# Down products in three f16 parts and reciprocals spread by transfers, in the second layer of a two-layer block

## The reference, cut to what matters

```python
# attention: 16 heads of 64 columns, causal
y = softmax(q k^T / 8) v ;  attn = y @ w_out
# experts: scores of a gate, the top 8 of 16 kept and normalized, one shared expert
hg = xn w_gate[e]^T ; hu = xn w_up[e]^T
h  = silu(hg) * hu
ye = h w_down[e]^T
y  = sum_e ye * combine[e]          # the shared expert with weight 1
out = x + attn + y
```

## Time and profile before

| | |
|---|---|
| median of 3 runs | 3251.74 us (3250.49 to 3253.42) |
| profiled execution | 3248.36 us, its span 3246.6 us |
| layer 0 | up to about 1243 us of the span |
| busy | PE 96%, DVE 62%, ACT 50%, POOL 39% |
| DMA | 259.86 MB, mean 80 GB/s |

### The profile page before, as it was taken

The page is one execution under the profiler, slowest core; times in us unless marked ns, Lnnn a source line. Parts: engine busy times, 40 slices in busy tenths (PEclk is TensorE's granted clock), DMA queues, the critical chain, the costliest instruction groups (busy, mean ns, idle before and its releaser), DMA issues.

```text
span 3246.6 us, 62545 instructions
## 1 busy us (share of the span) xinstructions
PE 3103.6 (96%) x23476; PEld 1674.8 (52%) x23476; DVE 2005.2 (62%) x3829; ACT 1632.8 (50%) x3433; POOL 1279.7 (39%) x1223
## 2 busy tenths in 40 slices
PE   4999999999999994999999999999999999999999
PEld 2565555655555652445555554554554554554554
DVE  5666666656666653666666666666666666666664
ACT  2666656556666663444444444444444444444443
POOL 1333333323333321444444444444444444444444
PEclk9999999999999996999999999999999999999999
DMA  4211122221222113332432432432432442432431
GB/s 116 53 50 50 50 59 63 62 50 50 62 50 52 50 47 107 105 96 76 108 103 71 108 104 71 108 105 70 108 103 72 108 107 68 108 107 68 108 105 43
DMA packets 239643, 259.86 MB, mean 80 GB/s; under 512 B 27248, under 2 KB 228080, under 8 KB 230640
## 3 DMA queue, kind: packets, MB, share of 16 engines
q1 hardware_dynamic: 217680, 239.12, 28.1%
q10 hardware_dynamic: 21664, 16.73, 1.7%
HBM read 107.91 MB, written 21.50 MB: 40 GB/s over the span
## 4 chain that ended last, share of the span: by engine, by line
PE 56%; DVE 2%; DMA 1%; SPq 1%; ACT 1%; POOL 0%; issue 0%; DVEq 0%; POOLq 0%; ACTq 0%
PE l_ps_out L1548 9%; PE l_ps_any L1585 7%; PE l_ps_any L1448 6%; PE l_ps_any L1450 6%; PE l_ps_any L1449 6%; PE l_ps_exp L1531 4%; PE l_ps_exp L1533 4%; PE l_ps_any L1591 3%; PE l_ps_any L1506 3%; PE l_ps_sum L1559 2%; PE l_ps_any L1571 2%; PE l_ps_exp L1535 2%; DMA l_spread<-route_scratch 1%; SPq L1089 1%; PE l_ps_any L1511 1%; PE l_ps_any L1442 1%
## 5 line engine op out<-in xcount | busy, mean ns | idle before, releaser
L1161 POOL TENSOR_TENSOR l_hw<-l_hidden,l_spread 128x512 f32<-128x512 f32 x256 | 325.5, 1277 | 761.5 <-DMA l_spread<-route_scratch 200.2
L614 DVE TENSOR_REDUCE neg_max<-ps_any 128x1 f32<-128x384 f32 (+3 forms) x704 | 417.4, 634 | 269.1 <-PE ps_any L728 264.6
L1249 ACT ACTIVATE l_probs<-l_ps_exp 128x512 f32<-128x512 f32 x640 | 376.9, 596 | 377.4 <-PE l_ps_exp L1535 288.0
L501 ACT ACTIVATE probs<-ps_exp 128x512 f32<-128x512 f32 x640 | 349.3, 602 | 155.2 <-PE ps_exp L743 154.5
L442 POOL TENSOR_SCALAR_AFFINE_SELECT probs<-probs 128x512 f32<-128x512 f32 x256 | 159.4, 634 | 597.4 <-ACT probs L501 597.4
L1370 DVE TENSOR_REDUCE l_neg_max<-l_ps_any 128x2 f32<-128x768 f32 (+2 forms) x384 | 316.4, 863 | 86.4 <-PE l_ps_any L1511 86.0
L1531 PE MATMUL l_ps_exp<-l_q_a,l_k_a 128*128 128x512 f16 (+3 forms) x1024 | 306.4, 300 | 0.3 <-ACT l_probs L1249 0.2
L1548 PE MATMUL l_ps_out<-l_probs,l_v 128*64 128x512 f32 (+3 forms) x2048 | 303.1, 438 | 0.0
L1533 PE MATMUL l_ps_exp<-l_q_b,l_k_b 65*128 65x512 f16 (+3 forms) x1024 | 295.4, 300 | 0.0
L726 PE MATMUL ps_any<-k_st,q_st 120*128 120x128 f16 (+3 forms) x1024 | 252.8, 304 | 36.2 <-DMA k_st<-stack_scratch 35.2
L1256 ACT ACTIVATE l_tanh<-l_ps_any 128x512 f32<-128x512 f32 x272 | 162.4, 597 | 208.2 <-PE l_ps_any L1450 113.7
(11 more groups left out here) (234 smaller groups left out, 6276.1 us busy)
## 6 DMA issues: line engine op xcount, KB each, us to landing
l_spread<-route_scratch SPq DMA_DIRECT2D x64, 1024.0 KB, 5.5
l_q_a<-l_q_hi SPq DMA_DIRECT2D x256, 128.0 KB, 2.4
l_q_b<-l_q_lo SPq DMA_DIRECT2D x128, 128.0 KB, 2.4
l_k_a<-l_k_hi SPq DMA_DIRECT2D x128, 128.0 KB, 2.4
l_k_a<-l_k_lo SPq DMA_DIRECT2D x128, 128.0 KB, 2.4
l_k_b<-l_k_hi SPq DMA_DIRECT2D x128, 128.0 KB, 2.4
q_st<-rot_hi SPq DMA_DIRECT2D x64, 128.0 KB
k_st<-rot_hi SPq DMA_DIRECT2D x64, 128.0 KB
```

The source lines that it names most:

```text
L501: nc.scalar.activation(probs[:, n % 2, u], ps_exp[:, (10 * g + u) % 3], ACT.Exp, scale=float(HD0 + DR) ** -0.5).then_inc(exp_done.sem, 1)
L614: nc.vector.tensor_reduce(neg_max[:, n % 2, heads[0]:heads[0] + k, t], src, AX.X, ALU.max, negate=True).then_inc(drained["dve"], 1)
L1161: nc.gpsimd.tensor_tensor(dst, hidden[:, k % 2], spread[:, c % 2, n % CHUNK], ALU.mult).then_inc(hw_ok.sem, 1)
L1249: nc.scalar.activation(probs[:, n % 2, u], ps_exp[:, (5 * p + u) % ST_BANKS], ACT.Exp, scale=float(HD1) ** -0.5).then_inc(exp_done.sem, 1)
```

## The change

The down weights are split as the gate and up weights are, and `hw` holds two f16 halves. A new step `hw n` comes behind POOL's multiplication: ACT writes the high half, DVE subtracts it from the f32 value and writes the low half. `down` then has three f16 products for each expert, and DVE divides by the weights' scale of 64 while it adds. One ring of five f32 tiles, `hid`, takes the place of `tanh`, `gated` and `hidden`, and is written in place. Routing weights come in chunks of two experts with three buffers.

`rec_lo` and `spread` are gone. `rec_out s` writes the reciprocals of four pairs to DRAM (128 KB), `rec_in` reads those of two pairs back, each row broadcast to the 64 partitions of its head (two transfers of 256 KB) into one buffer, and `divide n` is a DVE product of `yT` with it. The list ORDER1 is another one; the steps are as listed.

```diff
+SPREAD = 2
+HID_SLOTS = 5
 ORDER1 = (
...
+    ("spread_in", 0, 4), ("exp", 0, 0, 3), ("exp", 0, 0, 4), ("rec_in", -1, 2), ("sums", -1, 6), ("rec", -1, 1),
+    ("sums", -1, 7), ("v", 0, 3, 0), ("values", -1, 7), ("max", 0, 1, 0), ("max", 0, 1, 1), ("exp", 0, 1, 0),
+    ("exp", 0, 1, 1), ("max", 0, 1, 2), ("exp", 0, 1, 2), ("max", 0, 1, 3), ("values", 0, 0), ("max", 0, 1, 4),
+    ("up_in", 0, 5), ("gate_in", 0, 6), ("exp", 0, 1, 3), ("up_in", 0, 6), ("v", 0, 0, 1), ("turn_max", 0, 1),
+    ("qk", 0, 2, 0), ("gate_in", 0, 7), ("divide", -1, 4), ("qk", 0, 2, 1), ("exp", 0, 1, 4), ("sums", 0, 0),
+    ("divide", -1, 5), ("hw", 0, 5), ("hw", 0, 6), ("up_in", 0, 7), ("exp", 0, 2, 0), ("qk", 0, 2, 2),
+    ("exp", 0, 2, 1), ("qk", 0, 2, 3), ("exp", 0, 2, 2), ("exp", 0, 2, 3), ("max", 0, 2, 0), ("hw", 0, 7),
+    ("down", 0, 1), ("max", 0, 2, 1), ("gate_in", 0, 8), ("up_in", 0, 8), ("divide", -1, 6), ("exp", 0, 2, 4),
+    ("exp", 0, 3, 0), ("values", 0, 1), ("max", 0, 2, 2), ("gate_in", 0, 9), ("rec_in", -1, 3), ("up_in", 0, 9),
+    ("res", -1), ("exp", 0, 3, 1), ("max", 0, 2, 3), ("load", 1), ("norm", 1), ("hw", 0, 8), ("exp", 0, 3, 2),
+    ("divide", -1, 7), ("sums", 0, 1), ("spread_in", 0, 5), ("hw", 0, 9), ("exp", 0, 3, 3), ("values", 0, 2),
...
+    ("rec_out", 0, 0), ("down", 0, 2), ("hw", 0, 12), ("qk", 0, 3, 2), ("qk", 0, 3, 3), ("exp", 0, 4, 2),
+    ("rec", 0, 0), ("exp", 0, 4, 3), ("gate_in", 0, 14), ("v", 0, 3, 1), ("exp", 0, 4, 4), ("hw", 0, 13),
...
+    ("exp", 0, 7, 1), ("exp", 0, 7, 2), ("gate_in", 1, 4), ("exp", 0, 7, 3), ("max", 1, 0, 4), ("values", 0, 6),
+    ("spread_in", 1, 2), ("qk", 1, 1, 0), ("exp", 0, 7, 4), ("turn_max", 1, 0), ("hw", 1, 1), ("out", 0, 0),
...
+    ("v", 1, 2, 0), ("qk", 1, 1, 3), ("rec_out", 0, 1),
 )
...
+        rec_dram = nc.dram_tensor("rec_scratch", [2, P, T // 2], F32, kind="Internal").ap()
...
-        w_d = sb("w_d", [P, EXPERTS, D])
+        w_d = sb("w_d", [P, 2, EXPERTS, D], F16)
...
-        rec_p = sb("rec_p", [P, 2, T // 2], F16)
-        spread = sb("spread", [P, 2, CHUNK, T])
+        y_rec = sb("y_rec", [P, 2, 2, T // 2])
+        spread = sb("spread", [P, 3, SPREAD, T])
...
-        tanh = sb("tanh", [P, 2, T])
-        gated = sb("gated", [P, T])
-        hidden = sb("hidden", [P, 2, T])
-        hw = sb("hw", [P, HW_SLOTS, T])
+        hid = sb("hid", [P, HID_SLOTS, T])
+        hw = sb("hw", [P, HW_SLOTS, 2, T], F16)
...
-        split_late = [(w_g, w_g_in), (w_u, w_u_in)]
+        split_late = [(w_g, w_g_in), (w_u, w_u_in), (w_d, w_d_in)]
...
+                if name == "rec_out":
+                    k = 2 * b + n
+                    sp.wait_ge(rec_ok.sem, rec_ok.at(k, 2))
+                    if k >= 2:
+                        release(sp, sp_passed)
+                        sp.wait_ge(rec_in.sem, rec_in.at(2 * k - 2, 0))
+                    sp.dma_start(rec_dram[k % 2], rec[:]).then_inc(rec_out.sem, 16)
+                if name == "rec_in":
+                    k = 4 * b + n
+                    sp.wait_ge(rec_out.sem, rec_out.at(k // 2, 16))
+                    if k:
+                        release(sp, sp_passed)
+                        sp.wait_ge(y_div.sem, y_div.at(2 * k, 0))
+                    rows = rec_dram[k // 2 % 2].rearrange("(r f j) q -> r f j q", r=2, f=2)
+                    for r in range(2):
+                        sp.dma_start(y_rec[HD1 * r:HD1 * r + HD1],
+                                     rows[r, :, 2 * (n % 2):2 * (n % 2) + 2].partition_broadcast(HD1)
+                                     ).then_inc(rec_in.sem, 16)
...
+                if name == "hw":
+                    k = EXPERTS * b + n
+                    if k >= HW_SLOTS:
+                        b_old, e_old = divmod(k - HW_SLOTS, EXPERTS)
+                        filling(act, f"d{b_old}_{chunk_of(e_old)}")
+                    act.wait_ge(weighted.sem, weighted.at(k, 1))
+                    nc.scalar.activation(hw[:, k % HW_SLOTS, 0], hid[:, k % HID_SLOTS], ACT.Copy).then_inc(hw_hi.sem, 1)
...
-                if name == "spread":
-                    bank = full(dve, f"spread{b}_{n}")
-                    dve.wait_ge(y_ok.sem, y_ok.at(PAIRS * b + n, 1))
-                    nc.vector.scalar_tensor_tensor(out=yT[:, n], in0=bank, scalar=1.0 / REC_SCALE, in1=yT[:, n],
-                                                   op0=ALU.mult, op1=ALU.mult).then_inc(drained["dve"], 1)
+                if name == "divide":
+                    p = PAIRS * b + n
+                    dve.wait_ge(y_ok.sem, y_ok.at(p, 1))
+                    dve.wait_ge(rec_in.sem, rec_in.at(p // 2, 32))
+                    y = yT[:, n].rearrange("p (f q) -> p f q", f=2)
+                    nc.vector.tensor_tensor(y, y, y_rec[:, :, n % 2], ALU.mult).then_inc(y_div.sem, 1)
...
+                if name == "hw":
+                    k = EXPERTS * b + n
+                    dve.wait_ge(hw_hi.sem, hw_hi.at(k, 1))
+                    nc.vector.tensor_tensor(hw[:, k % HW_SLOTS, 1], hid[:, k % HID_SLOTS], hw[:, k % HW_SLOTS, 0],
+                                            ALU.subtract).then_inc(hw_ok.sem, 1)
...
-                        ins = pe.matmul(out, w_d[:, e], hw[:, k % HW_SLOTS], start=(e == todo[0]), stop=(e == todo[-1]))
+                        for cw, cx in ((0, 0), (0, 1), (1, 0)):
+                            ins = pe.matmul(out, w_d[:, cw, e], hw[:, k % HW_SLOTS, cx],
+                                            start=(e == todo[0] and cw + cx == 0), stop=(e == todo[-1] and cw == 1))
```

More of the change, by code:

```diff
@@ new lines @@
+    ("scale", 1), ("max", 0, 2, 4), ("sums", 0, 2), ("out", -1, 1), ("turn_max", 0, 2), ("exp", 0, 3, 4),
+    ("gate_in", 0, 10), ("outT", -1), ("up_in", 0, 10), ("spread_in", 0, 6), ("qk", 0, 3, 0),
+    ("gate_in", 0, 11), ("exp", 0, 4, 0), ("hw", 0, 10), ("exp", 0, 4, 1), ("up_in", 0, 11), ("qk", 0, 3, 1),
+    ("xnT", 1), ("gate_in", 0, 12), ("up_in", 0, 12), ("sums", 0, 3), ("spread_in", 0, 7), ("hw", 0, 11),
+    ("route", 1), ("v", 0, 1, 1), ("gate", 1), ("gate_in", 0, 13), ("v", 0, 2, 1), ("up_in", 0, 13),
@@ new lines @@
+    ("rec_out", 0, 0), ("down", 0, 2), ("hw", 0, 12), ("qk", 0, 3, 2), ("qk", 0, 3, 3), ("exp", 0, 4, 2),
+    ("rec", 0, 0), ("exp", 0, 4, 3), ("gate_in", 0, 14), ("v", 0, 3, 1), ("exp", 0, 4, 4), ("hw", 0, 13),
+    ("max", 0, 3, 0), ("values", 0, 3), ("max", 0, 3, 1), ("exp", 0, 5, 0), ("sums", 0, 4), ("max", 0, 3, 2),
+    ("exp", 0, 5, 1), ("rec_in", 0, 0), ("exp", 0, 5, 2), ("max", 0, 3, 3), ("divide", 0, 0), ("up_in", 0, 14),
+    ("gate_in", 0, 15), ("values", 0, 4), ("max", 0, 3, 4), ("qk", 1, 0, 0), ("lat", 1), ("hw", 0, 14),
@@ new lines @@
+    ("exp", 0, 5, 3), ("turn_max", 0, 3), ("up_in", 0, 15), ("divide", 0, 1), ("rec_in", 0, 1), ("cT", 1),
+    ("gate_in", 0, 16), ("exp", 0, 5, 4), ("qk", 1, 0, 1), ("qk", 1, 0, 2), ("hw", 0, 15), ("up_in", 0, 16),
+    ("divide", 0, 2), ("qk", 1, 0, 3), ("v", 1, 0, 0), ("gate_in", 1, 0), ("divide", 0, 3), ("spread_in", 1, 0),
+    ("values", 0, 5), ("max", 1, 0, 0), ("exp", 0, 6, 0), ("up_in", 1, 0), ("hw", 0, 16), ("gate_in", 1, 1),
+    ("max", 1, 0, 1), ("sums", 0, 5), ("spread_in", 1, 1), ("up_in", 1, 1), ("exp", 0, 6, 1), ("gate_in", 1, 2),
@@ L874 @@
+    ("exp", 1, 0, 0), ("down", 1, 0), ("exp", 1, 0, 1), ("hw", 1, 4), ("qk", 1, 1, 2), ("exp", 1, 0, 2),
+    ("v", 1, 2, 0), ("qk", 1, 1, 3), ("rec_out", 0, 1),
 )
@@ L899, in filled_by1 @@
         return [f"{name}{b}"]
-    if name in ("turn_max", "spread", "out"):
+    if name in ("turn_max", "out"):
         return [f"{name}{b}_{step[2]}"]
@@ L1007, in layer1 @@
         route_out = sig("route_out", 16)
-        spread_in = [sig(f"spread_in{n}", 16) for n in range(2)]
+        spread_in = [sig(f"spread_in{n}", 16) for n in range(3)]
+        rec_out = sig("rec_out", 16)
+        rec_in = sig("rec_in", 32)
         stored = sig("stored", 16)
```

109 lines of the change are left out of this document (41 added, 68 removed).

## The result

The changed kernel takes 3314.28 us (median of 4 runs, 3308.88 to 3322.03) against 3252.58 before: ratio 1.0191, 95% interval 1.0169 to 1.0213. It is 1.9% slower where 2.5% faster was forecast, and it lies outside the range. The profiled execution took 3313.75 us, its span is 3312.0.

The account below looks back on a forecast made before the run. PE's work was taken to bound the kernel: 3248.4 - 125.9 + 2.4 (start) + 11 (end) + 32 (new PE waits) = 3167.9, with 3.4 up to the median 3171 us; range 3136 to 3232.

Parts of the forecast that it names:

- PE's saving: Second layer: f16 down products save 56.8 us, dropped spread matmuls 69.1; PE loses 125.9 us, 7.9 a period, leaving 112.9.
- DVE's load: DVE's work per sequence, with 25 new two-input operations, goes from 76.7 to 97.5 us of 112.9.
- halts: Standstills of DVE's new two-input instructions beside a running POOL instruction: 0 to 0.88 us each, 0.44 taken.
- the prediction's other bound: By the Trainium skill page, a DVE halt could last POOL's whole longest instruction, 1.81 us, not 0.88.
- 2 us of new PE waits on each sequence, 32 us: Second layer: DVE backlog above 3.5 us makes PE wait 2 us a sequence, bounds 0 and 6.
- The backlog walk: Step by step through both orders, DVE durations added, PE's taken off: backlog reaches 4.6, 4.1 and 3.7 us, 3.5 carried.
- That is DVE time (5 us a sequence), not PE time at first: DVE stands at three divides for reads of the reciprocals, 2.5, 1.2 and 1.2 us; PE hardly feels it.
- passed on: Rival: waits behind hw(0,7) and DVE's 5 us at transfers reach PE, 5.5 us a sequence, 3227 us; chance 0.20.
- The rival that ended slower: Rival: DVE becomes the bound through halts of 0.88 us on all 25 operations, period 121.2, 3272 us; chance 0.10.
- POOL waits for a transfer now and PE doesn't feel it: Routing weights in halved spread_in chunks with three buffers: POOL's wait for them costs PE nothing.
- Start: PE's first gate product, waiting 7.39 us for a low half, waits for a third one, w_d: +2.4 us.
- End: Last sequence: nothing covers the new chain of reciprocals, transfers and divides; +11 us, 7 to 15.

Follow-up runs that it names:

- s4: Both parts put into the old kernel's step order, reciprocal products on DVE, low-half subtractions on POOL and placed later: 3193.3 us, ratio 0.9811 to the kernel before.
- e5: e4 with POOL's weightings and key sums replaced by memsets, so POOL reads nothing in SBUF: 3126.9 us, ratio 0.9613 to the kernel before.
- e4: Changed kernel without the reciprocals' transfers, and with ACT's copy and DVE's subtraction reading hid unweighted, not waiting for POOL: 3197.9 us, ratio 0.9818.
- e2: Changed kernel without the write and reads of the reciprocals; y_rec holds ones, the eight products stay: 3220.4 us, ratio 0.9903 to the kernel before.
- e3: Changed kernel with POOL's weighted product written to an unread tile, so copy and subtraction read hid unweighted: 3291.9 us, ratio 1.0116 to the kernel before.
- h1: Old kernel's order with only the reciprocals by transfers (two y_rec buffers, early reads, products on DVE), down products still f32: 3229.0 us, ratio 0.9927.
- r2: h1 with the eight products with the reciprocals on POOL in place of DVE: 3213.7 us, ratio 0.9884 to the kernel before.

## Why the prediction was wrong

- **PE's saving: right to within a us.** The 112.9 us forecast were a period that still held the 0.5 us of waits from before; PE's work was to go from 120.3 to 112.4. It is 113.0 in s4 and 112.8 in e5. In the changed kernel it is 114.4, 2.0 more than forecast, of which the granted clock of 0.99 in place of 1.00 in s4 explains about 1.1; I had such a loss only at the end.
- **DVE's load: over-priced, and not what bounds.** 97.5 us forecast, 1107.07/1500 x 124.4 = 91.8 measured; halts of 0.26 to 0.30 us on the mean in place of 0.44. The mean subtraction was to be near 1.1 us and is 0.946. Yet the halts cost PE up to 4.2 us a period (e4 to e5), at a smaller mean than I took, and the longest goes beyond the 0.88 us that I took from the rows as the most: 2.07 - 0.69 = 1.38 us (the prediction's other bound was 1.81).
- **The step that failed: "2 us of new PE waits on each sequence, 32 us".** It is 10.0 less 0.5, so 9.5, nearly five times as much. The 7.5 us over the forecast and the 2.0 by which PE's work is longer make 9.5 us a period; fifteen of them are 143 us, what lies between 3171 and 3314. The backlog walk took DVE's work off PE's from zero and gave DVE no waits of its own. In truth DVE comes to each drain after its own waits, for the reads and for ACT: 13.3 us of standing a sequence that the walk counted as capacity.
- **"That is DVE time (5 us a sequence), not PE time at first": wrong.** I had the three places, but took 2.5, 1.2 and 1.2 us for divide(-1,6), divide(0,0) and divide(0,2), which are 3.3, 2.8 and 2.0 in one sequence, and passed on 0.1 us. It is 8.3 on the mean, and e2 shows 5.0 of it in the period. Part of the size is the transfer: 4.4 us to landing for my 2.9. I took 2.9 from a plain read of 256 KB. That these reads spread each row over 64 partitions isn't shown to be the reason, as the same plain read takes 5.1 in the changed kernel:
```profile
l_x_res<-x_scratch SPq DMA_DIRECT2D x16, 256.0 KB, 5.1
```
- **The hw chain was no line of the sum**, only part of a rival ("passed on", 3227, given 0.20). That rival had both mechanisms right and the size too small: 5.5 us a sequence for 9.5. The rival that ended slower (3272) had the period at 121.2 by load; no run shows DVE full.
- **"POOL waits for a transfer now and PE doesn't feel it": unproved.** POOL stands 122.9 us of 1500 for spread in the changed kernel; e3, which took POOL's product out of the chain, gives 22 us.
- **Start: right.** Forecast +2.4, measured 9.72 - 7.39 = 2.33:
```profile
1297.96 0.61 PE L1468 MATMUL l_ps_any<-l_xn_p,l_w_g 128*128 128x512 f16 x1 [9.72 <-DVE l_w_d L1304]
```
- **End: near.** Forecast +11; +8.1 from the last L1431 on. From the last sums to the end of the last out product it is 3287.0 to 3306.3, 19.3 us (17.1 forecast, 11.3 before), in the order forecast, with PE idle at both reads:
```profile
3288.94 0.33 SPq L1126 DMA_DIRECT2D rec_scratch<-l_rec  x1
...
3296.22 3.75 PE L1600 MATMUL l_ps_any<-l_yT,l_w_out 128*128 128x512 f32 x4 [6.91 <-DVE l_yT L1409]
...
3302.55 3.78 PE L1600 MATMUL l_ps_any<-l_yT,l_w_out 128*128 128x512 f32 x4 [2.57 <-DVE l_yT L1409]
```

## What to carry to other kernels

When every engine's queue is in order and PSUM banks are few, a new wait costs by what is queued behind it, not by the share of its engine that is busy: with DVE busy 74% of the time (68% of the whole span) this kernel lost 10 us a period. A walk through the order must give the second engine its own waits and start each of its steps at the later of the two. Put an operation that waits for a transfer or for a two-engine chain onto the queue where nothing urgent is behind it, and place it late: 17 subtractions moved to POOL and placed a little later gave 101 us in one order, and moved without a change of place they cost 17 in the other. Try the parts of a change in the order that worked: one of the two parts alone (h1, r2) was a gain, and both with the subtractions on another engine (s4) are 1.9%.
